# Group 1's weight preparation spread over the first unit, and two row tiles normalised on ScalarE

## What is computed

```python
ln_out = _ln(hidden_states, ln_w, ln_b)
q = _fp8_linear_pertensor(ln_out, wq, wq_scale, q_in_scale)   # also qx, k, v
q = _ln(q, qln_w, qln_b)
core = _gqa(q, k, v)
kx, vx = split(einsum(cond, w_kv_x)); xout = _gqa(qx, kx, vx)
cat = concatenate([core, xout]); catq = _div_clamp_fp8(cat, proj_smooth)
x = x + tanh(g_xattn) * einsum(catq, wproj) * (proj_in_scale * proj_w_scale)
x = x + tanh(g_ffn) * ffn(_layernorm(x))        # top 2 of 8 experts
```

## Time and profile before

| what | value |
|---|---|
| median of 3 runs | 717.48 us (716.75 to 718.15) |
| profiled execution, its own time | 719.06 us |
| its span, first to last instruction | 717.3 us |
| around the span | 1.76 us |
| busy: PE, DVE, ACT, POOL | 644.7, 602.9, 548.0, 460.1 us |
| mean granted TensorE clock | 0.965 |

### The profile page before, as it was taken

The page is one execution under the profiler, slowest core; times in us unless marked ns, Lnnn a source line. Parts: engine busy times, 40 slices in busy tenths (PEclk is TensorE's granted clock), DMA queues, the critical chain, the costliest instruction groups (busy, mean ns, idle before and its releaser), DMA issues. The chain is left out here.

```text
span 717.3 us, 14819 instructions
## 1 busy us (share of the span) xinstructions
PE 644.7 (90%) x4548; PEld 589.8 (82%) x4549; DVE 602.9 (84%) x1379; ACT 548.0 (76%) x1923; POOL 460.1 (64%) x636
## 2 busy tenths in 40 slices
PE   1677999999999999999999999999976569999994
PEld 0577889999998999999899999999965448888883
DVE  7579899999999999998999998987876697776771
ACT  4787979998988998998899899888854136656660
POOL 4666677687777778877777787787643124545442
PEclk9989999999999999999999999999999659999998
DMA  6100100010020101002010110100392512232322
GB/s 218 59 1 31 60 1 30 2 59 31 1 61 1 31 2 60 31 1 60 1 32 3 51 42 1 60 1 2 120 397 100 179 64 45 45 58 44 58 31 29
DMA packets 35509, 37.72 MB, mean 53 GB/s; under 512 B 2704, under 2 KB 30352, under 8 KB 35440
## 3 DMA queue, kind: packets, MB, share of 16 engines
q1 hardware_dynamic: 31024, 30.84, 13.0%
q0 software_dynamic: 4416, 6.03, 5.2%
HBM read 31.62 MB, written 5.24 MB: 51 GB/s over the span
## 5 line engine op out<-in xcount | busy, mean ns | idle before, releaser
L1192 POOL TENSOR_SCALAR shared<-shared,rsum 128x256 f32<-128x256 f32 x256 | 143.5, 573 | 67.1 <-DVE rsum L856 61.7
L615 ACT ACTIVATE shared<-s,nmax 128x256 f32<-128x256 f32 x256 | 122.5, 498 | 34.3 <-DVE nmax L851 34.2
L861 DVE TENSOR_TENSOR pt_lo<-t,pt_hi 128x512 fp32r<-128x512 f32 x128 | 86.9, 679 | 9.2 <-ACT pt_hi L621 8.3
L1186 POOL TENSOR_TENSOR rstd<-rstd,half 128x7 f32<-128x7 f32 (+1 forms) x64 | 91.2, 1425 | 5.3
L851 DVE TENSOR_REDUCE nmax<-s 128x2 f32<-128x512 f32 x128 | 86.6, 678 | 5.3 <-PE s L364 4.6
L375 PE MATMUL t<-ident,shared 128*128 128x128 f32 x512 | 78.0, 275 | 8.8 <-DVE pt_lo L861 5.6
L621 ACT CAST pt_hi<-t 128x512 fp32r<-128x512 f32 x128 | 76.4, 597 | 12.3 <-PE t L375 10.0
L629 ACT ACTIVATE shared<-route_bank,head_w 128x512 f32<-128x512 f32 (+1 forms) x124 | 81.6, 690 | 0.3 <-PE route_bank L389 0.3
L846 DVE TENSOR_TENSOR qk_lo<-shared,qk_hi 128x512 fp32r<-128x512 f32 x96 | 78.5, 817 | 3.0 <-POOL qk_hi L1201 1.9
L364 PE MATMUL s<-qk_hi 128*128 128x256 f32 x256 | 78.0, 305 | 0.6 <-ACT shared L615 0.6
L320 PE MATMUL pj_a<-w_ring,xq 128*128 128x256 f32 x488 | 73.8, 295 | 2.2 <-DVE w_ring L927 2.2
(11 more groups left out here) (255 smaller groups left out, 1927.9 us busy)
## 6 DMA issues: line engine op xcount, KB each, us to landing
expert_w<-in_w SPq DMA_DIRECT2D x24, 512.0 KB, 9.3
spare<-in_wT SPq DMA_DIRECT2D x19, 256.0 KB, 3.0
wp_raw<-in_wpT SPq DMA_DIRECT2D x16, 256.0 KB, 2.9
spare<-in_wkvT SPq DMA_DIRECT2D x16, 128.0 KB, 3.1
spare<-in_wT SPq DMA_DIRECT2D x9, 128.0 KB, 3.2
spare<-in_x SPq DMA_DIRECT2D x1, 1024.0 KB, 5.6
x_hat<-acc SPq DMA_DIRECT2D x1, 1024.0 KB, 4.7
out<-spare SPq DMA_DIRECT2D x1, 1024.0 KB, 7.9
```

Of the source, the lines that this page charges most:

```text
L615: e = act.activation(probs[:, st, h * S:(h + 1) * S], s_bank[st][:, h * S:(h + 1) * S], ACT.Exp, bias=nmax[:, st, h:h + 1], accum_out=psum ...
L861: dve.tensor_tensor(pt_lo[:, :, c], pt_bank[:].rearrange("p (n s) -> p n s", n=4), pt_hi[:, :, c].bitcast(F32), ALU.subtract).then_inc(ptl ...
L1186: pool.tensor_tensor(rstd[:, st, c], rstd[:, st, c], half[:, c], ALU.pow).then_inc(rstd_ready, 1)
L1192: m = pool.tensor_scalar(probs[:, st, c], probs[:, st, c], rsum[:, st, h:h + 1], 1.0, ALU.mult, ALU.mult)
```

## The change

On DVE, `row_normalise(1)` goes; ACT does it, as `row_scale(1)`, after the first eight `affine_in` and before the first weight casts, and POOL makes the shift for it. Group 1's weights are summed, and half 0 centred, between the rests of v0 and `normalise_q(0, 0, 0)`; the first four blocks of half 1 follow before `normalise_q(0, 0, 1)`, and the later ones after the second `split_heads`. The casts stand in ACT's stream after `square(2)` and after `affine_in(19)`, the rests in DVE's after `row_sum(0, 0, 1)` and `row_sum(0, 1, 1)`. In `prepare` nothing is left for group 1. PE's and SP's streams stay as they are.

```diff
@@ ScalarE
+            def row_scale(c):
+                act.wait_ge(ln_shift, c)
+                for t in range(*chunks[c]):
+                    m = act.activation(acc[:, t, :], acc[:, t, :], ACT.Identity, scale=lnr[:, t:t + 1], bias=ln_mr[:, t:t + 1])
+                m.then_inc(z_ready, 1)
             for n in range(8):
                 affine_in(n)
+            row_scale(1)
             weights_hi(0, 0, 2)
...
             square(1)
-            act.wait_ge(ln_shift, 1)
...
-            m.then_inc(z_ready, 1)
+            row_scale(2)
             split_ctx(2)
             square(2)
+            weights_hi(1, 1, 0)
+            weights_hi(1, 1, 1)
             affine(0, 0, s_bank[0])
...
             for n in range(16, 20):
                 affine_in(n)
+            weights_hi(1, 1, 2)
+            weights_hi(1, 1, 3)
             exps(0, 0, 0)
...
             def prepare(g, b, place):
-                if g + 1 < G and b < 2:
-                    c = 2 * b + place if g > 0 else (b - 1) * 9 + 2 * place
-                    for n in ((c,) if g > 0 else (c, c + 1)):
-                        if 0 <= n < 4:
-                            weights_hi(g + 1, (g + 1) % 2, n)
+                if 0 < g < G - 1 and b < 2:
+                    weights_hi(g + 1, (g + 1) % 2, 2 * b + place)
@@ VectorE
             quantise_in(0, 4)
-            row_normalise(1)
             weights_lo(0, 0, 2)
...
             dve.tensor_tensor(v0_w[:, 1], v0_raw, v0_w[:, 0].bitcast(F32), ALU.subtract).then_inc(v0_ready, 1)
+            for k in range(KT):
+                sum_weights(1, k)
+            centre_weights(1, 0, (0, 1, 2, 3) + later_blocks(1))
             normalise_q(0, 0, 0, early_banks[0][0])
             normalise_kv(0, 0, 0, early_banks[0][1])
+            centre_weights(1, 1, (0, 1, 2, 3))
             normalise_q(0, 0, 1, early_banks[1][0])
             normalise_kv(0, 0, 1, early_banks[1][1])
             ctx_rest(2)
             split_heads(0, 0, 0)
             split_heads(0, 0, 1)
+            centre_weights(1, 1, later_blocks(1))
             split_heads(0, 0, 2)
...
             row_sum(0, 0, 1)
+            weights_lo(1, 1, 0)
+            weights_lo(1, 1, 1)
             probs_lo(0, 0, 0)
...
             row_sum(0, 1, 1)
-            for k in range(KT):
-                sum_weights(1, k)
-            centre_weights(1, 0, (0, 1, 2, 3))
+            weights_lo(1, 1, 2)
+            weights_lo(1, 1, 3)
             normalise_q(2, 2, 0, o_bank)
...
             rest_v0(1, s_bank[1])
-            centre_weights(1, 0, later_blocks(1))
...
             def prepare(g, par, b, place):
-                centring = 1 if g == 0 else 0
-                if place in (0, 2) and g + 1 < G and b == centring:
+                if place in (0, 2) and 0 < g < G - 1 and b == 0:
                     centre_weights(g + 1, 1, (0, 1, 2, 3) if place == 0 else later_blocks(g + 1))
...
-                if place in (1, 3) and g + 1 < G and b < 2:
-                    for c in (((), (0, 1)), ((2,), (3,)))[b][place // 2] if g > 0 else ((0, 1), (2, 3))[place // 2]:
+                if place in (1, 3) and 0 < g < G - 1 and b < 2:
+                    for c in (((), (0, 1)), ((2,), (3,)))[b][place // 2]:
                         weights_lo(g + 1, 1 - par, c)
@@ GpSimd
-            def row_shift():
-                t = slice(*chunks[2])
-                pool.wait_ge(ln_rstd, 3)
+            def row_shift(c):
+                t = slice(*chunks[c])
+                pool.wait_ge(ln_rstd, c + 1)
...
             row_power(1)
+            row_shift(1)
             centre_first()
...
-            row_shift()
+            row_shift(2)
```

More of the change, by code:

```diff
@@ L702, in _ @@
             square(1)
-            act.wait_ge(ln_shift, 1)
-            for t in range(*chunks[2]):
-                m = act.activation(acc[:, t, :], acc[:, t, :], ACT.Identity, scale=lnr[:, t:t + 1], bias=ln_mr[:, t:t + 1])
-            m.then_inc(z_ready, 1)
+            row_scale(2)
             split_ctx(2)
             square(2)
+            weights_hi(1, 1, 0)
+            weights_hi(1, 1, 1)
             affine(0, 0, s_bank[0])
@@ L1242, in row_power @@
                 pool.tensor_tensor(lnr[:, t], lnr[:, t], half[:, t], ALU.pow).then_inc(ln_rstd, 1)
-            def row_shift():
-                t = slice(*chunks[2])
-                pool.wait_ge(ln_rstd, 3)
+            def row_shift(c):
+                t = slice(*chunks[c])
+                pool.wait_ge(ln_rstd, c + 1)
                 pool.tensor_tensor(ln_mr[:, t], mv[:, t, 0], lnr[:, t], ALU.mult).then_inc(ln_shift_part, 1)
-                pool.wait_ge(ln_shift_part, 1)
+                pool.wait_ge(ln_shift_part, c)
                 pool.tensor_scalar(ln_mr[:, t], ln_mr[:, t], -1.0, 1.0, ALU.mult, ALU.mult).then_inc(ln_shift, 1)
```

## The result

The changed kernel takes 715.82 us (median of 20 runs, 713.83 to 716.89) against 717.42 us for the kernel before (20 runs): a ratio of 0.9975, 95% interval 0.9965 to 0.9984. That is 1.6 us less by the medians and 1.8 by the ratio, where the forecast was 5.4.

A forecast was written before the change was run, and what follows sets the result against it. PE was taken as the bound from 115 us on, so only its earlier waits and slow clock could go: 1.24 + 2.86 + 1.4 + 0.63 + 0.28 = 6.4 us, less 1.0 charged, leaves 5.4: 712.1 us, range 709.9 to 716.3.

The forecast's parts named there:

- Tiles 2 and 3: Before the first projection: DVE loses L947, so PE starts at about 18.9 instead of 20.17; gain 1.24 us, bounds 0 and 1.9.
- Sums and half 0: Unit 0, ahead of L810: group 1's sums and centring, 4.1 us, fit DVE's 4.66 us idle time without a wait.
- Half 1's centring: Unit 0: four blocks, 1.10 us, in 1.90 idle; later blocks, about 0.75 us, in 1.37; both end before the releaser.
- Rests: Unit 0: DVE's two pairs of group 1 pieces may make POOL slip; charged 0.4 us each, bounds 0 and 1.2 each.
- Power beside centring: Unit 0: POOL's `power` gets in between DVE's centring instructions; charged 0.2 us in all, bounds 0 and 2.3.
- Unit 1: Removing group 1's work there shortens PE's waits by 2.86, 0.63 and 0.28 us, and a faster clock gives 1.4.
- the centring step: Unit 1: with centring ahead of L810 removed, L810 moves from 66.31 to 63.45; 2.86 us of PE's 3.26 go.
- the clock's 1.4 us: After PE's shortened 3.26 us wait the clock stays at 1.00 instead of half; worth 1.4 us, other bound 0.
- Rival A: Unit 0: all pieces behind the first gap fall on the path, 4.35 us; gain 2.1, time 715.4; chance 0.16.
- C: Unit 0: DVE's added work keeps POOL out and POOL stretches it; 9.35 against 6.4, +2.9, time 720.4; chance 0.06.

The follow-up runs named there:

- c1: The kernel before, unchanged, run again for a second profile; 717.48 us.
- e1: The changed kernel with tiles 2 and 3 normalised on VectorE again, group 1's weights staying early; 715.17 us, ratio 0.9970 to the kernel before.
- e2: The kernel before with only tiles 2 and 3 moved to ScalarE; 716.15 us, ratio 0.9996 to the kernel before.
- e6: The changed kernel with statistics of tiles 4 to 7 between VectorE's roundings and its rests of group 0's weights; 714.57 us, ratio 0.9967 to before.
- e5: The changed kernel with group 1's sums and half 0's centring ahead of VectorE's wait for v0's cast; 714.20 us, ratio 0.9964 to before.
- e3: The changed kernel with VectorE's four rests of group 1's weights back at unit 1's end; 714.24 us, ratio 0.9971 to before.
- e4: The changed kernel with GpSimd's two rests of group 0's output weights moved from unit 0 into unit 1; 715.69 us, ratio 0.9987 to before.

## Why the prediction was wrong

The marks below are starts of `normalise_q`'s instruction (L810, L816) in VectorE's timelines, less the start of the first weight sum.

| `normalise_q` of unit, half | c1 (before) | changed | difference |
|---|---|---|---|
| 0, first | 20.45 | 21.43 | +1.0 |
| 0, second | 23.83 | 24.82 | +1.0 |
| 1, first | 33.64 | 34.69 | +1.05 |
| 1, second | 42.10 | 44.02 | +1.9 |
| 2, first | 48.46 | 51.28 | +2.8 |
| 2, second | 55.85 | 56.11 | +0.3 |
| 3, first | 64.85 | 63.92 | -0.9 |

At unit 4 (ScalarE's L644) the difference is 116.7 - 118.3 = -1.6, about what the medians say. That it agrees so well is partly luck: the time behind this mark differs by 1 us between these two profiles (587.1 against 588.2).

- **Tiles 2 and 3, forecast a gain of 1.24: the first step that failed.** I took L927 to start 1.24 us earlier and to keep its 3.30 us, and named as lower bound "0, if POOL's widening becomes the releaser". It became the releaser and slipped by 2.7 us (6.32 against 3.65), so the projection comes 0.84 us later. The bound excluded a loss, and nothing in the rows excluded one. L947 had served as a place where GpSimd got in. e1 and e2 show it, and e6 shows that another stretch of single-input work does the same. ScalarE's part was free, as forecast: its two activations took 1.12 us and its casts start 4.51 us from the first sum, as before (4.52).
- **Sums and half 0, forecast free in 4.66 us: the second step that failed, and the one that the first normalisation shows.** They took 3.5 us and ended 2.1 us after `rstd` was ready. The idle time was a difference between two engines, and both ends moved. VectorE came later: v0's cast stands behind the squares of the projection, so `v0`'s rest starts 17.55 us from the first sum instead of 16.74. GpSimd was ready earlier, at 19.33 instead of 20.42. That left 1.4 us of room, where even c1 has only 2.96. The row part alone makes this normalisation 1.3 us earlier, although its projection is late (e2, 19.13); group 1's work then takes 2.3 us. With the sums ahead of the wait it comes at 18.69 (e5). The two steps together make +1.0 instead of -1.2.
- **Half 1's centring: right.** The distance between the marks does not change there (+1.0, +1.0, +1.05).
- **Rests, charged 0.4 each: mis-sized.** They cost 0.9 and 0.9, from GpSimd's rows 0.85 and 0.94. e3 takes these back in GpSimd's rows, but not in the marks of its own profile, where the half clock comes in. I had written that GpSimd could slip by up to 1.2, and then charged a third of it.
- **Power beside centring, charged 0.2: right in size.** The powers took 1.73 and 1.48 us, against 1.49 and 1.48 in c1. The one that grew ran beside the sums; the one beside the centring did not grow. The row of 2.50 us was the right warning, in the wrong place: I set it against centring, and it applied to the widening.
- **Unit 1, forecast 2.86 + 1.4 + 0.63 + 0.28 = 5.2 us: nearly right.** From the mark at +2.8 to that at unit 4, -1.6, is 4.4 us; the centring step alone gave 2.5 (+2.8 to +0.3). Of the clock's 1.4 us only part can be real gain: the half clock that goes from 66 us comes in at 53 us.

In sum, unit 0 was to end at -0.2 (1.24 gained, 1.0 charged) and ended at +2.8, 3.0 us worse, and unit 1 gave 0.8 us less than its 5.2. That accounts for the 3.8 us between the 5.4 of the forecast and the 1.6 of the profiles. Rival A (715.4) named nearly the right time, but only in part the reason: it had the pieces behind the first gap fall on the path by their own length, and they lengthened GpSimd's work instead, while the piece in the first gap, which A left free, was the one that ran over. C's mechanism, GpSimd kept out, is there, but at the widening and not at the powers, and the whole loss is about a third of C's 9.35 us. (C's sum also counts eleven blocks where fourteen moved, which would make it 0.5 us larger.)

What stays open: why e4's earlier units are not seen in its times, what part of each difference the clock makes, and what decides between taking turns and standing still when GpSimd meets a row of VectorE's instructions. The variants have their half-clock stretches in different places of unit 0, and the runs of one kernel spread over 2 to 6 us.

## What to carry to other kernels

An idle time is a difference between two engines; before filling it, ask whether the same change moves either end, and look whether a second profile shows it at the same size. When an instruction leaves VectorE's stream, look at what GpSimd was doing beside it. Here roundings followed without a break by two-input instructions kept GpSimd waiting until the row ended, and a stretch of statistics or of row scaling between the two, at no extra work, let it through. Bounds for a step that shortens one queue have to include a loss wherever two engines have been seen to lengthen each other's instructions.

## What the runs showed of the hardware that I had not expected

- One GpSimd widening of 0.6 us lasted 4.41 us while VectorE ended its roundings and issued five two-input instructions back to back. The Trainium skill, page "SBUF — State Buffer", section "Who interferes with whom", gives the shared ports to whoever issues first, for the whole instruction. If that were all, GpSimd could have had its turn at the next of VectorE's instructions, which start 0.6 us apart. The runs show it held over several instructions in a row, every time in that order (6.31 or 6.32 us for the four widenings in all eight profiles that have it), and 3.65 to 3.70 us in the other orders, where the last widening took turns with the rests.
- The same instruction in the same kernel took 2.50 us in one execution and 0.35 in another.
- TensorE's half-clock stretches moved between kernels that differ by a microsecond or two in their waits: in the changed kernel one appeared at 53 us as the one at 66 us vanished.
